# GpSimd's order in the first stage of a decoder kernel, and the mask's products in row halves

## The reference

```python
x = x + _L0_attn_ref(_layernorm(x), W_Q, W_K, W_V, W_O, b_Q, b_K, b_V, b_O)   # 16 heads of 128
x = x + _L0_xattn_ref(_layernorm(x), ctx_512, ctx_512)
x = x + _L0_ffn_ref(_layernorm(x), ln1_w, ln2_w, Wq, Wk, Wv, Wo, A, B, W_in_base, W_up_base, W_down)
x = x + _L1_attn_ref(_layernorm(x), W_mem, conv_k, W_q, theta, ...)
x = x + _L1_xattn_ref(_layernorm(x), ctx_512, ctx_512, q_norm_w, k_norm_w, w_out)
x = x + _L1_ffn_ref(_layernorm(x), gate_W_packed, gate_scales, up_W_packed, ...)
```

## Time and profile before

| | |
|---|---|
| median of three runs | 1754.83 us (1753.07 to 1756.31) |
| the profiled execution | 1752.43 us |
| its span, first to last instruction | 1750.6 us |
| stage 1 | from the start to about 561 us |
| s3a, sixteen steps | about 719 to 822 us |
| s5a, sixteen steps | about 1361 to 1445 us |
| PE busy over the span | 91% |

### The profile page before, as it was taken

How to read it: one execution, slowest core, us unless ns; L and a number is a source line. 1 busy time by engine, 2 the same in 40 slices (tenths; PEclk the granted TensorE clock), 3 DMA queues, 4 the chain that set the end, 5 groups by cost and what they waited for, 6 DMA issues and landing times. The chain is left out here.

```text
span 1750.6 us, 37012 instructions
## 1 busy us (share of the span) xinstructions
PE 1584.9 (91%) x14664; PEld 1281.7 (73%) x14664; DVE 1089.3 (62%) x1734; ACT 863.5 (49%) x1466; POOL 672.5 (38%) x527
## 2 busy tenths in 40 slices
PE   6999999999996887899999797899997898999998
PEld 4888888888885565777788564566664675888887
DVE  5777677677776888566442568999994565112111
ACT  3555555555453565555422346667672674222222
POOL 0111211211212663531422265999994430232332
PEclk9999999999998999899999799999998898999999
DMA  3011111111112300010102120000000900000000
GB/s 105 16 64 55 40 63 60 33 63 60 37 59 78 109 2 26 8 12 10 40 1 105 28 64 1 1 2 1 2 1 26 360 17 1 1 13 12 1 12 12
DMA packets 72351, 70.26 MB, mean 40 GB/s; under 512 B 24816, under 2 KB 64368, under 8 KB 71840
## 3 DMA queue, kind: packets, MB, share of 16 engines
q1 hardware_dynamic: 72224, 68.46, 12.2%
HBM read 46.03 MB, written 19.27 MB: 37 GB/s over the span
## 5 line engine op out<-in xcount | busy, mean ns | idle before, releaser
L665 POOL TENSOR_TENSOR s_w_parts<-s_w_raw,s_w_parts 128x768 fp32r<-128x768 f32 x15 | 27.8, 1855 | 401.9 <-ACT s_w_parts L615 401.9
L1488 DVE TENSOR_TENSOR s6f_hid<-s6f_act_sb,s6f_u_ps 128x512 f32<-128x512 f32 x64 | 44.0, 688 | 218.4 <-PE s6f_u_ps L1439 218.4
L1511 POOL TENSOR_TENSOR s6f_hid_parts<-s6f_hid,s6f_hid_parts 128x512 fp32r<-128x512 f32 x64 | 82.7, 1291 | 224.3 <-ACT s6f_hid_parts L1477 224.3
L2228 POOL TENSOR_TENSOR s4b_with_q<-s4b_with_q 128x1024 f32<-128x1024 f32 x64 | 150.8, 2378 | 0.4 <-DVE s4b_with_q L2183 0.4
L2183 DVE TENSOR_TENSOR s4b_with_q<-s4b_c_ps,s_q_rows 128x2048 f32<-128x2048 f32 x64 | 146.1, 2285 | 1.2 <-PE s4b_c_ps L2322 1.1
L598 PE MATMUL s_o_ps<-s_w_parts,s_zT 128*128 128x256 f32 x768 | 110.6, 294 | 4.1 <-DVE x_rows L701 4.1
L539 PE MATMUL s_v_ps<-s_wv_parts,s_xnT 128*128 128x256 f32 x768 | 104.6, 286 | 8.2 <-ACT s_v L644 6.8
L1477 ACT ACTIVATE s6f_hid_parts<-s6f_hid 128x512 fp32r<-128x512 f32 x64 | 40.5, 632 | 144.5 <-PE s6f_o_ps L1459 141.0
L539 PEld LDWEIGHTS s_v_ps<-s_wv_parts,s_xnT 128*128 128x128 f32 x768 | 97.0, 191 | 13.8 <-ACT s_v L644 10.0
L1459 PEld LDWEIGHTS s6f_o_ps<-s6w_parts,s6f_hid_parts 128*128 128x128 f32 x768 | 99.2, 188 | 6.8 <-issue 1.0
L598 PEld LDWEIGHTS s_o_ps<-s_w_parts,s_zT 128*128 128x128 f32 x768 | 97.3, 193 | 8.8 <-issue 4.5
(11 more groups left out here) (333 smaller groups left out, 3982.0 us busy)
## 6 DMA issues: line engine op xcount, KB each, us to landing
stored_weights<-s1q_halves SPq DMA_DIRECT2D x16, 768.0 KB, 3.7
s6w_parts<-stored_weights SPq DMA_DIRECT2D x32, 384.0 KB, 7.6
s1q_packed<-in_codes SPq DMA_DIRECT2D x8, 384.0 KB, 4.4
s1q_scale<-in_scale_rows SPq DMA_DIRECT2D x8, 384.0 KB, 4.9
s3p_raw<-in_ffn_pieces SPq DMA_DIRECT2D x8, 384.0 KB, 8.5
early_values<-s_vbd SPq DMA_DIRECT2D x1, 2176.0 KB, 12.3
s_vbd<-early_values SPq DMA_DIRECT2D x4, 544.0 KB, 7.0
x_rows<-in_x SPq DMA_DIRECT2D x4, 512.0 KB, 5.4
```

What stands on the lines that cost most here:

```text
L1488: nc.vector.tensor_tensor(hid[:, f % 2, :], act_sb[:, f % 2, :], u_ps[:, f % 2, :], ALU.mult) \
L1511: nc.gpsimd.tensor_tensor(hid_parts[:, f % 2, 1, :], hid[:, f % 2, :], hid_parts[:, f % 2, 0, :], ALU.subtract).then_inc(low_done, 1)
L2228: nc.gpsimd.tensor_tensor(with_q[:, half, :, 0, :, n_, :], with_q[:, half, :, 0, :, n_, :], with_q[:, half, :, 1, :, 1 - n_, :], op).then_ ...
```

## The change

There are two edits. On GpSimd in stage 1, turn h now holds the low part of piece h-2, then the sum of piece h-1, then `split_low(h)`. In both attentions the mask's product for bank j uses 64 rows of the two tiles in place of 128: rows 0 to 63 for even j, rows 64 to 127 for odd j. For that `ident_r` holds, in each half of its rows, the 64 by 64 identity twice side by side, so that 64 rows give the mask for all 128 output rows; VectorE fills it with two copies in place of one.

```diff
-                run_steps(pool, H, [(split_low, 0), (lambda j, rnd, slot: deq.gpsimd_sum(j), 1),
-                                    (lambda j, rnd, slot: deq.gpsimd_low(j, slot), 2)])
+                run_steps(pool, H, [(lambda j, rnd, slot: deq.gpsimd_low(j, slot), 2),
+                                    (lambda j, rnd, slot: deq.gpsimd_sum(j), 1), (split_low, 0)])
...
-            nc.vector.tensor_copy(ident_r[:, :], core.c("ident")).then_inc(masks, 1)
+            for b in range(2):
+                rows = slice(b * S, (b + 1) * S)
+                last = nc.vector.tensor_copy(ident_r[rows, :].rearrange("p (a s) -> p a s", a=2),
+                                             core.c("ident")[rows, rows].unsqueeze(1).to_broadcast([S, 2, S]))
+            last.then_inc(masks, 1)
...
                 for j in range(4):
-                    nc.tensor.matmul(s_ps[:, j, 0:4 * S].rearrange("p (h s) -> p h s", s=S), ident_r[:, :],
-                                     mask_r[:, :].unsqueeze(1).to_broadcast([P, 4, S]), start=True, stop=False)
+                    half = slice(j % 2 * S, (j % 2 + 1) * S)
+                    nc.tensor.matmul(s_ps[:, j, 0:4 * S].rearrange("p (h s) -> p h s", s=S), ident_r[half, :],
+                                     mask_r[half, :].unsqueeze(1).to_broadcast([S, 4, S]), start=True, stop=False)
```

## The result

The changed kernel takes 1736.49 us, the median of four runs (1736.16 to 1738.81), against 1754.62 us (1753.07 to 1756.31, four runs) for the kernel before: a ratio of 0.990, with a 95% interval of 0.988 to 0.992. It is 18.1 us faster; forecast were 1739 us and some 16 us. The profiled execution of after is the slowest of its four, 1738.81 us with a span of 1737.0 us, and that of before was faster than its median, so the two profiles lie only 13.6 us apart.

What follows compares the result with a forecast made beforehand. PE, busy for 91% of the span, was taken as the bound. 1752.43 - 7.9 - 0.7 - 7.5 = 1736.3 us for the profiled execution, plus 2.4 to the runs' median: 1738.7, said as 1739; range 1733 to 1749.

Steps and rivals of the forecast that it cites:

- (a): Stage 1, GpSimd's sum ahead of split_low: DVE's 15 waits and PE's 7 for the values' copy go, 7.9 us.
- my upper bound of 8.0: Stage 1, most the earlier sum could gain: six times 1.10 us and once 1.10 plus 0.3.
- (b): GpSimd's low part first in the turn: 0 in stage 1's steady part, tail 0.7 us shorter.
- my 2: Stage 1, the 2 us in hand between the values' copy (about 155.6) and PE wanting the bank (157.72).
- (c): Both attentions, mask in row halves: two load rounds for four, 0.235 us less per step, 7.5 us over 32 steps.
- (d): Two copies for ident_r in place of one, done well before the mask's first product: 0 us.
- A: Rival, attentions: mask halves take turns or shape change eats the saving; only stage 1 gains, 1746 us; chance 0.12.
- B: Rival, stage 1: PE's wait returns behind another, or the earlier store hinders weight loads; 1747 us; chance 0.08.
- C: Rival, attentions: halves don't overlap and products wait for each other, 0.5 us more per step, 1762 us; chance 0.05.
- D: Rival, whole kernel: nothing to be seen, as more falls to 1.2 GHz (1.7 us each) eat the gain; chance 0.07.

Runs made afterwards that it cites:

- mask only: Kernel before with only the mask's product in row halves, GpSimd's order as before: 1746.84 us, ratio 0.996, 8.0 us faster.
- order only: Kernel before with only GpSimd's new order in stage 1 (low part, sum, split_low), old mask: 1743.18 us, ratio 0.994, 11.7 us faster.
- low first: Kernel before with GpSimd's turn as low part, split_low, sum; mask as before: 1744.73 us, ratio 0.994, 10.2 us faster.
- sum first: Kernel before with GpSimd's turn as sum, split_low, low part; mask as before: 1745.18 us, ratio 0.994, 9.7 us faster.
- one half: Changed kernel, but all four mask products use rows 0 to 63: 1747.26 us, ratio 0.997 against the kernel before.

## Why the prediction was right

**(a) The sum.** The mechanism was the one forecast: sum at once after the second `over` (done at 144.4 by the forecast and at 143.50 measured, 144.44 with the 0.94 us by which this place stands earlier), L2484 stretched beside it (forecast 2.4, measured 2.42 at the median), no wait of DVE, no wait of PE, L539 behind L557 by 1.37. The size can be read from the distance between the starts of DVE's L687 eight units apart, which is two heads and holds one of PE's lost 1.10 us:

| kernel | steady part, us per 8 units |
|---|---|
| before | 64.73 and 64.75 at first, then 65.03 |
| mask only | 64.68 to 64.84 |
| after | 63.81 to 63.92 |
| order only | 63.50 to 63.55 |
| low first | 63.28 to 63.86 |
| sum first | 63.48 to 63.78 |

Between rows of the same pace of PE (see the last section) it is 65.03 - 63.84 = 1.19 us and 64.70 - 63.50 = 1.20 us; I had 1.10. Over seven such distances that is 8.3 us, a little over my upper bound of 8.0. Where the other 0.09 us are isn't known. The turn L580 near the end of the stage comes 8.76 us earlier, where (a) and (b) together were put at 7.9 + 0.7 = 8.6. Of that, 0.7 is lost at once: the next L589 takes 1.91 us and not 1.20 as in before, because there the granted clock, by its record in the trace, stays at 1.2 GHz until 558.8 us, where in before it was back at full from 551.5. So the stage ends 8.0 us earlier, at 553.5, where I had said near 552.

One detail of (a) was wrong, without effect. I had L2489 meet L669 and take about 1.3 us; at the place shown both start at 149.40, and GpSimd's L669 was the one to be stretched, from 1.28 to 2.11 us. In other pieces L2489 takes up to 1.91. The exponent comes at 151.82, or 152.76 with the 0.94 us, where I had 153.9, so there was 1 us more in hand than my 2.

A second one is about attribution. I gave the whole gain to the sum's place and put the low part's at 0 in the steady part. Low first shows that this was wrong: it keeps all 15 waits for the sum, and PE's waits are gone. PE's wait came from the whole stall of DVE, 3.65 us of waiting and 1.6 us of hold-up by the low part, of which only 1.1 us came through to PE. I had computed that L2484 of before began only at the end of GpSimd's low part, and did not ask what its 1.6 us would be worth alone. In this kernel the answer changes nothing in the sum, as both moves were made; with the sum's move left out, the forecast would have been wrong by all of 8 us.

**(b) The tail.** Forecast 0.7 us. L693 there has 0.42 us in place of 1.15, and PE's wait shrinks from 2.91 to 2.27, 0.64 us. Sum first, which leaves the low part last, keeps 2.9. What I didn't have: the low part, now earlier, meets L2478, which takes 1107 ns and not 555, in 14 of the 16 pieces. I had put 0.3 us at most there. The distances from one L687 to the next are the same in order only, which has this too, and in sum first, where this instruction keeps its 0.55 us, so it costs nothing that shows. The unit of L2484, stretched by the sum, is the one that got longer on DVE, 7.56 us where before has 6.92; the distance over eight units doesn't show that either, since the next unit makes it up.

**(c) The mask.** Forecast 0.67 to 0.43 us, two rounds of 0.117 fewer, 0.235 per step. Measured 0.67 to 0.43, and the pair of steps of s3a 6.76 and 7.27 to 6.52 and 7.03, 0.24 each. s5a gains 3.7 us by the windows, 16 x 0.235 being 3.76. s3a gains 5.1; the 1.3 us beyond go with the clock, which before had 0.98 and after 1.00, just the one stretch at 1.2 GHz that the earlier trace rows had shown. The runs part the two: mask only has that stretch too and gains 3.6 us in s3a, order only lacks it and gains 1.5. The rule that different tiles load and multiply in parallel (the Trainium skill, "TensorEngine Tiling (Array Packing)", Key Properties) holds here, and the kernel with one half shows that the gain comes from it and not from fewer rows.

**(d) Two copies.** Those of s3a start at 706.0 and 707.5 us and the last is done by 708, 3.6 us ahead of the mask's first product at 711.5. No wait for them in either attention. As forecast.

**The rivals.** A would have left the group at 0.67; that is what one half does, and two halves don't. B would have left PE a wait for L644; there is none, in low first and sum first neither. C would have made the group longer than 0.9. D was real in kind and small in size: a gain of 16.1 us between the profiles was forecast and 13.6 measured. Stage 1 and the attentions gained 16.8; the stages that the change doesn't touch lost 3.2. The trace's record of the granted clock has 123.5 us of the span at 1.2 GHz against 100.0 before, and order only, mask only, low first and sum first have 107 to 110 us. That these stretches fall elsewhere because the stages begin at other times is argued, not shown.

**The spread.** The forecast was 2.5 us above the measured median (1739 against 1736.49). Two things of that size vary from run to run: the clock, above, and a second one in PE's own pace in stage 1, below. Order only gained 11.7 us where stage 1's terms make 8.6; its profiled run had the quicker of the two paces nearly throughout. The runs can't tell a cause of 3 us from these, so that the median came this close is in part luck.

## What to carry to other kernels

Of an engine's long list of waits only that part counts which comes through to the bound engine: here 43.7 us of DVE's waits were worth 1.2 us per two heads, and each of the two moves that took that much from the one chain got all of it, also the one that left every wait in place. Where a small product contracts over a broadcast or repeated operand, put successive ones on different row halves of the array: four went from 0.67 to 0.43 us, in both orders of the halves that were tried, and nothing was gained by fewer rows alone. Before moving a product earlier, look who empties its bank, and where that stands in its own engine's list.

## What the runs showed of the hardware

**Who stretches whom.** Where DVE and GpSimd held each other up, the one that began later got longer, as far as the starts tell them apart, and that wasn't always DVE: beside the sum L2484 took 2.42 us for 0.95; beside the low part L2478, an int32 operation with one tensor input, took 1.107 us for 0.555; L669 took 2.11 for 1.28. L2478 hadn't been expected, having no second input from SBUF. It wasn't so for all: L701 and L682, which read one of their inputs from PSUM, ran beside L665 and kept their 1.21 and 0.75 us.

**Two paces of PE.** A unit with values takes 9.07 us or 9.16 us with the same instructions and the same granted clock, and changes from one to the other within a run: in after, six groups of eight units have it at 9.16 and then the last at 9.07; in order only it is six at 9.07 and the last at 9.16. That is 0.34 us per eight units, up to 2.5 us over the stage. Most of it is in the two halves of the values' products, which take 1.50 and 1.42 us from start to the next group in place of 1.46 and 1.39. No wait in the trace goes with it, and what causes it stays open.

**The clock.** In the first 24 us of s5a the granted clock was 0.50, the lower of the two levels (1.2 GHz), in the kernel with one half, and 0.80 over the first 23.5 us in before. By the record of the granted clock it fell some 4 to 5 us ahead of s5a's first mask product in all nine profiles, and rose again after 13.7 us in eight of them and after 30.7 us in this one. That made s5a 6 us longer with a mask that costs the same. A single profile can mislead by nearly as much as either edit is worth.
